# Two middle phases of a four-batch transformer kernel reordered: early maxima, one norm on GpSimd, fillers spread anew

## The reference, cut to what matters

```python
q, k, v = heads(_ln(x) @ Wq + bq), heads(ctx @ Wk + bk), heads(ctx @ Wv + bv)   # 16 heads of 8
x = x + merge(softmax(q @ k.T * 8**-0.5) @ v) @ Wo + bo        # attention 0
h = _ln(x); x = x + relu(h @ Ws1)**2 @ Ws2 + routed(h)         # truncated top-2 weights: routed part is zero save where a weight is 1
x = x + softmax((_ln(x) @ Wq1 + bq1) @ (ctx @ Wk1 + bk1).T) @ (ctx @ Wv1 + bv1)   # attention 1, one head
p = softmax(_ln(x) @ Ws + bs).T                                # 8 experts; each takes its 256 best tokens
x = x + scatter_add(topk(p, 256) * (gelu(xin @ W1 + b1) @ W2 + b2))
```

## Time and profile before

| what | us |
|---|---|
| median of three runs (lowest, highest) | 214.19 (213.75, 217.28) |
| the profiled execution's own time | 214.98 |
| its span | 213.2 |
| busy: TensorE, VectorE, ScalarE, GpSimd | 185.8, 133.1, 90.4, 100.8 |
| mean granted clock of TensorE | 0.983 |

### The profile page before, as it was taken

One profiled execution on the slowest core, in us unless ns is written; L12 is line 12 of the kernel. 1 busy time (PEld: TensorE's weight loads), 2 busy tenths in 40 slices (PEclk: granted clock), 3 DMA queues, 4 the chain that ended last, 5 costly groups with the idle time before them and its releaser, 6 DMA issues.

```text
span 213.2 us, 3647 instructions
## 1 busy us (share of the span) xinstructions
PE 185.8 (87%) x1254; PEld 111.6 (52%) x1254; DVE 133.1 (62%) x457; ACT 90.4 (42%) x219; POOL 100.8 (47%) x111
## 2 busy tenths in 40 slices
PE   6888997997989989899999999799788989987970
PEld 2544542433532556348577675433266867766860
DVE  5787789129791998958778788888742552212110
ACT  2423872242632565134843644356855323333320
POOL 0599638000208002650217748700077887888652
PEclk9999998899999999999999999999999999999996
DMA  6635222101100001049940021110012233323223
GB/s 191 184 82 144 72 51 51 38 8 50 44 0 3 0 0 49 2 143 282 337 134 3 15 88 55 61 40 0 3 44 37 41 48 38 41 39 50 26 29 35
DMA packets 16127, 13.64 MB, mean 64 GB/s; under 512 B 3699, under 2 KB 13079, under 8 KB 16103
## 3 DMA queue, kind: packets, MB, share of 16 engines
q1 hardware_dynamic: 12246, 10.62, 16.4%
q0 software_dynamic: 2944, 2.30, 7.6%
q10 hardware_dynamic: 913, 0.43, 0.8%
HBM read 8.03 MB, written 3.21 MB: 53 GB/s over the span
## 4 chain that ended last, share of the span: by engine, by line
PE 44%; DVE 21%; POOL 12%; issue 9%; DMA 7%; ACT 4%; POOLq 1%; DVEq 0%; ACTq 0%
POOL out L1968 8%; PE psum L1024 8%; DVE mrow L1542 6%; DMA out<-pT,idx 5%; PE psum L921 3%; DVE pT L1689 3%; POOL pT L1960 3%; PE psum L931 3%; PE psum L1042 3%; DVE stats L1424 2%; PE psum L994 2%; PE psum L965 2%; PE psum L947 2%; PE psum L1105 2%; PE psum L1061 2%
## 5 line engine op out<-in xcount | busy, mean ns | idle before, releaser
L1858 POOL TENSOR_SCALAR ve<-mv 128x4 f32<-128x4 f32 (+1 forms) x19 | 4.4, 230 | 72.0 <-DVE mv L1427 71.9
L784 ACT ACTIVATE pT<-psum 103x512 f32<-103x512 f32 (+1 forms) x36 | 21.2, 595 | 31.9 <-PE psum L996 31.8
L1968 POOL DMA_INDIRECT out<-pT,idx x16 | 25.5, 1594 | 8.6 <-issue 4.0
L921 PE MATMUL psum<-c 128*128 128x512 bf16 x108 | 27.6, 379 | 1.0 <-ACT key_map L809 1.0
L1542 DVE TENSOR_REDUCE mrow<-psum 128x8 bf16<-128x616 f32 x32 | 24.6, 789 | 5.0 <-PE psum L965 5.0
L1960 POOL DMA_INDIRECT pT<-gather_rows,idx x16 | 16.9, 1057 | 21.1 <-DVE idx L1747 16.8
L1762 DVE SCALAR_TENSOR_TENSOR pT<-psum,pT 128x128 f32<-128x128 f32 x16 | 5.1, 347 | 26.1 <-PE psum L1380 18.3
L1366 PE MATMUL psum<-xinT,w 128*128 128x256 f32 (+1 forms) x80 | 16.5, 349 | 3.9 <-ACT xinT L866 3.9
L871 ACT ACTIVATE pT<-psum,b 128x256 f32<-128x256 f32 (+1 forms) x40 | 15.0, 431 | 8.2 <-PE psum L1366 7.4
L1380 PE MATMUL psum<-w,pT 128*128 128x128 f32 x128 | 17.7, 284 | 0.6 <-ACT pT L871 0.2
L1569 DVE RECIPROCAL rden<-psum 128x512 f32<-128x512 f32 (+1 forms) x5 | 13.6, 2716 | 6.7 <-PE psum L1024 6.0
(11 more groups left out here) (201 smaller groups left out, 377.4 us busy)
## 6 DMA issues: line engine op xcount, KB each, us to landing
w<-in_L_ffn_W SPq DMA_DIRECT2D x16, 256.0 KB, 6.0
gather_rows<-xrow SPq DMA_DIRECT2D x4, 272.0 KB, 2.1
x<-in_x SPq DMA_DIRECT2D x4, 256.0 KB, 4.1
q_stack<-q_hi SPq DMA_DIRECT2D x32, 32.0 KB, 1.8
out<-res SPq DMA_DIRECT2D x4, 256.0 KB, 2.1
q_stack<-q_lo SPq DMA_DIRECT2D x24, 32.0 KB, 1.8
b_rows<-in_L_ffn_b SPq DMA_DIRECT2D x1, 512.0 KB, 3.9
pT<-gather_rows,idx POOLq DMA_INDIRECT x16
```

Of the source, the lines that this page charges most:

```text
L784: nc.scalar.activation(pT[0:n, b % 2, s, :], ST_ps[s % 2][0:n, :], ACT.Exp).then_inc(exp_done, 1)
L921: pe.matmul(bank[b][:, :], ident16, c16[:, 0:4 * P], start=True, stop=True)
L1968: nc.gpsimd.indirect_dma_start(flat, bass.IndirectOffsetOnAxis(idx[:, h, e:e + 1], 0), y[:, e, h, :], None, bounds_check=last_row, oob_is_ ...
```

## The change

All edits are in the opening and in the phases' order; what is computed stays the same.

- Opening: `prep_q(1)` moves from behind the sixth score piece to behind the eighth and the second turn; fillers 4, 3, 1, 3, 3, 3 before the third to eighth piece; the six at the end go.
- Phase one: two 256-column fillers at slots 10 and 11; VectorE's `ln0_stats(3)` leaves. Six fillers before the last turn that opens phase two.
- Phase two: score pieces 0 and 1 of batch two at slot 0, 2 at slot 1, then 3 to 7 at slots 5, 7, 8, 9, 10, with their maxima in the same slots; three maxima so stand before `normalise`. `ln0_stats(3)` stands behind the first of them. The norm of batch three is GpSimd's (`norm(3)`). `prep_T(3)` and `prep_q(3)` move from slots 1, 2 to 4, 5, `q_low(3)` to slot 6, values to slot 8, `project` and the steps behind it one slot later (`moments2` stays), the once-only products one or two slots later. Fillers: two of 512 columns at slot 3, one at each of 8 to 11.
- Phase three: pieces 0 and 1 at slot 0, 2 at slot 1, 3 to 7 at slots 5, 6, 7, 9, 10; maxima 0 and 1 before `normalise`, the third behind it; values at slot 6; fillers: two of 512 columns at slots 3 and 4, one and two of 256 at slots 9 and 10.

```diff
+HEAD_WARM = {2: 4, 3: 3, 4: 1, 5: 3, 6: 3, 7: 3}
...
+PIECE_SLOTS = {0: {4 + u: (u,) for u in range(PAIRS)},
+               1: {0: (0, 1), 1: (2,), 5: (3,), 7: (4,), 8: (5,), 9: (6,), 10: (7,)},
+               2: {0: (0, 1), 1: (2,), 5: (3,), 6: (4,), 7: (5,), 9: (6,), 10: (7,)}}
+MAXIMA_SLOTS = {0: PIECE_SLOTS[0], 1: PIECE_SLOTS[1], 2: {0: (0, 1), 2: (2,), 5: (3,), 6: (4,), 7: (5,), 9: (6,), 10: (7,)}}
+TURN_SLOTS = {0: {9: (0, 1), 11: (2,)}, 1: {10: (0, 1), 11: (2,)}, 2: {8: (0, 1), 10: (2,)}}
+
+FILL = {0: {}, 1: {3: (2, 7), 8: (1, 4), 9: (1, 4), 10: (1, 4), 11: (1, 4)}, 2: {3: (2, 7), 4: (2, 7)}}
+FILL_HALF = {0: {10: 2, 11: 2}, 1: {}, 2: {9: 1, 10: 2}}
+STEP_SLOTS = {"project": (6, 5, 5), "turn": (7, 6, 6), "hidden": (8, 7, 7), "shared": (10, 9, 9), "moments1": (6, 6, 6), "moments2": (10, 10, 10)}
...
         def prep_slot(b):
-            return 4 if b == 0 else 1
+            return 4
         def values_slot(b):
-            return 2 if b == 0 else 3
+            return (2, 8, 6, 3)[b]
...
-                    warm_head(3)
+                    warm_head(HEAD_WARM[u])
...
-                if u == 5:
-                    prep_q(1)
                 if u % 2 == 1 and u >= 5:
                     maxima_T(0, (u - 5) // 2)
+            prep_q(1)
             maxima_T(0, J - 2)
             pe.wait_ge(ld_neg, 16)
-            warm_head(6)
...
                     if s == 0:
+                        if b == 1:
+                            warm_prep(6)
                         maxima_T(b, J - 1)
...
+                    if b in (1, 2) and s == 0:
+                        scores(b + 1, 0)
...
-                        if b == 1 and s == 4:
-                            pe.wait_ge(once_done, 5)
-                            warm(5, 4)
-                        if s >= 4:
-                            scores(b + 1, s - 4)
...
+                        if s in FILL[b]:
+                            n, to = FILL[b][s]
+                            if to == 4:
+                                pe.wait_ge(once_done, 6)
+                            if to == 7:
+                                pe.wait_ge(mT_done, b + 1)
+                            warm(n, to)
+                        if s in FILL_HALF[b]:
+                            pe.wait_ge(q_lo_done, min(b + 3, B))
+                            pe.wait_ge(v8_done, b + 1)
+                            warm_prep(FILL_HALF[b][s])
+                        for u in PIECE_SLOTS[b].get(s, ()):
+                            if b == 0 or u > 0:
+                                scores(b + 1, u)
+                        for j in TURN_SLOTS[b].get(s, ()):
+                            maxima_T(b + 1, j)
...
-                            if b + 2 < B:
-                                warm(4, 0)
...
-                            if b == 1:
-                                ln0_apply(3)
...
+                        early = b >= 1 and s < 2
+                        if b + 1 < B and early:
+                            for u in MAXIMA_SLOTS[b].get(s, ()):
+                                maxima(b + 1, u)
+                                if (b, u) == (1, 0):
+                                    ln0_stats(3)
+                        t = ph - 1
+                        if t >= 0 and s == 2:
+                            normalise(t, t, 0, J)
+                        if b + 1 < B and not early:
+                            for u in MAXIMA_SLOTS[b].get(s, ()):
+                                maxima(b + 1, u)
+                        if b == 0 and s == prep_slot(b) + 1:
                             q_low(b + 2)
...
-                        if b + 3 < B and s == 8:
-                            ln0_stats(b + 3)
...
+                        if b == 1 and s == step_slot(ph, "moments1"):
+                            q_low(b + 2)
...
+            def norm(b):
+                pool.wait_ge(xnT_ps_done[0], b)
+                pool.wait_ge(rstd_done[0], b + 1)
...
             for ph in range(B):
+                if ph == 1:
+                    ln_rstd(0, 3, 3)
+                    norm(3)
...
-                if ph + 3 < B:
-                    ln_rstd(0, ph + 3, ph + 3)
```

More of the change, by code:

```diff
@@ L62, in halves_done, with step_slot @@
     return n // NG * E * SH + sum(h1 - h0 for _, h0, h1 in GROUPS[:n % NG + 1])
+PIECE_SLOTS = {0: {4 + u: (u,) for u in range(PAIRS)},
[6 more added lines that the diff above has]
+STEP_SLOTS = {"project": (6, 5, 5), "turn": (7, 6, 6), "hidden": (8, 7, 7), "shared": (10, 9, 9), "moments1": (6, 6, 6), "moments2": (10, 10, 10)}
+def step_slot(ph, step):
+    return STEP_SLOTS[step][ph - 1]
 def index_group(e):
@@ L802, in _ @@
                         nc.scalar.copy(b1[:], tail2_ps[:, 0:E * FC]).then_inc(once_done, 1)
-                    if b == 1 and s == 1:
+                    if b == 1 and s == 2:
                         act.wait_ge(once_ps_done, 4)
@@ L815, in _ @@
                     t = ph - 1
-                    if t >= 0 and s == 6:
+                    if t >= 0 and s == step_slot(ph, "turn"):
                         copy_T(1, t, tail1_ps[0])
-                    if t >= 0 and s == 7:
+                    if t >= 0 and s == step_slot(ph, "hidden"):
                         hidden(t, t, 0, J, tail1_ps)
@@ L1203, in _ @@
                         pe.transpose(tail2_ps[:, 0:E * FC], b1_rows[:], ident[0:E * FC, 0:E * FC]).then_inc(once_ps_done, 1)
-                    if b == 1 and s == 0:
+                    if b == 1 and s == 2:
                         pe.wait_ge(once_done, 3)
@@ L1211, in _ @@
                         pe.matmul(tail2_ps[:, P:2 * P], w_q[:, 1, :], centre[:], start=True, stop=True).then_inc(once_ps_done, 1)
-                    if b == 1 and s == 3:
+                    if b == 1 and s == 4:
                         pe.wait_ge(once_done, 4)
@@ L1215, in _ @@
                                   stop=True).then_inc(once_ps_done, 1)
-                    if b == 1 and s == 5:
+                    if b == 1 and s == 6:
                         pe.wait_ge(once_done, 5)
@@ L1219, in _ @@
                                   stop=True).then_inc(once_ps_done, 1)
-                    if t >= 0 and s == 5:
+                    if t >= 0 and s == step_slot(ph, "project"):
                         project(t, 0, J, tail1_ps)
-                    if t >= 0 and s == 6:
+                    if t >= 0 and s == step_slot(ph, "turn"):
                         residual_T(1, t, t, tail1_ps[0])
-                    if t >= 0 and s == 7:
+                    if t >= 0 and s == step_slot(ph, "hidden"):
                         hidden(t, 0, J, tail1_ps)
@@ L1227, in _ @@
                         attend_half(0, s - 5)
-                    if t >= 0 and s == 9:
+                    if t >= 0 and s == step_slot(ph, "shared"):
                         shared(t, 0, J, tail1_ps)
@@ L1604, in _ @@
                                 ln0_apply(2)
-                            if b == 1:
-                                ln0_apply(3)
-                        if b + 1 < B and s >= 4:
-                            maxima(b + 1, s - 4)
-                        if b + 2 < B and s == prep_slot(b) + 1:
+                        early = b >= 1 and s < 2
[11 more added lines that the diff above has]
+                        if b == 0 and s == prep_slot(b) + 1:
                             q_low(b + 2)
@@ L1620, in _ @@
                         t = ph - 1
-                        if t >= 0 and s == 2:
-                            normalise(t, t, 0, J)
-                        if t >= 0 and s == 5:
+                        if t >= 0 and s == step_slot(ph, "project"):
                             add_projection(t, t, 0, J, tail1_ps)
-                        if t >= 0 and s == 6:
+                        if t >= 0 and s == step_slot(ph, "moments1"):
                             stats1(t, t, 0, J)
+                        if b == 1 and s == step_slot(ph, "moments1"):
+                            q_low(b + 2)
                         if ph == B - 1 and s == 8:
                             normalise(B - 1, B - 1, 0, J // 2)
-                        if t >= 0 and s == 9:
+                        if t >= 0 and s == step_slot(ph, "shared"):
                             add_shared(t, t, 0, J, tail1_ps)
-                        if t >= 0 and s == 10:
+                        if t >= 0 and s == step_slot(ph, "moments2"):
                             stats2(t, t, 0, J)
@@ L1901, in _ @@
             ln_rstd(0, 1, 1)
[L1902 to L1906, removed]
+            def norm(b):
+                pool.wait_ge(xnT_ps_done[0], b)
+                pool.wait_ge(rstd_done[0], b + 1)
+                m = moments(0, b)
+                for j in range(J):
+                    ins = nc.gpsimd.tensor_scalar(xn[:, j, :], x[:, b * J + j, :], mv[:, m, j, 0:1], rstd[:, m, j:j + 1],
+                                                  ALU.subtract, ALU.mult)
+                ins.then_inc(xn_done, 1)
+            norm(1)
             pool.wait_ge(q_lo_done, 1)
```

## The result

The changed kernel takes 210.36 us (median of 4, 209.54 to 210.85), the kernel before beside it 215.44 (4 executions). The ratio is 0.986, with a 95% interval of 0.982 to 0.991: faster, by less than two per cent. (The ratio leaves out executions far above the fastest, here the one at 217.28 us, and with them part of those in which the clock fell.) From the medians of what remains, 210.36 against 214.19, one gets 0.982; the interval holds both. I had forecast 209.2 from 214.19, 2.3% less, with a range of 207.9 to 210.8; 0.986 of 214.19 is 211.3, outside it. The first trace of each agrees with the forecast far better than the timed ratio does: spans 208.5 and 213.2, 4.7 us or 2.2% less. What lies between the two is the subject of the experiments.

A forecast was written before the change was run, and what follows sets the result against it. TensorE and VectorE were taken to wait for each other in turn up to the search. Terms 1.0 + 0.3 + 1.7 + 1.7 + 0.3 = 5.0 us off the 214.19 us median gave 209.2, range 207.9 to 210.8.

The forecast's parts named there:

- Step 1: Opening: eight fewer fillers on the path and a later query projection of batch one win 1.0 us (0.8 to 1.15).
- Step 2: End of phase one: VectorE loses the moments, but TensorE's ten added fillers take nearly all back; 0.3 us (0 to 0.5).
- Step 3: Clock fall behind phase one's end goes; 1.7 us won, 0 if the clock falls all the same.
- my slowest sum: All steps at their lower bounds at once: 211.3 us.
- Step 4: Phase two's new order, with an earlier reciprocal and a new wait before the sixth score, wins 1.7 us (0.9 to 2.0).
- The marks: Phase two, from its start: reciprocal at 6.6 us, TensorE at the projection at 13.4; 1.4 us wait before the sixth score.
- The two terms of the sum: Phase two on TensorE: 0.6 us from busy time and 0.85 from idle time, giving 1.45.
- GpSimd's part: Phase two: batch three's norm moved off VectorE to GpSimd, done near 8 us with slack 1.7; wins nothing by itself.
- Step 5: Phase three's new order puts early maxima into VectorE's idle time, with more fillers; wins 0.3 us (-0.5 to 0.8).
- Rival one: Phases two and three: fillers and new waits eat the orders' gain, opening and clock remain; 211.7 us, chance 0.21.
- Rival four: Clock falls elsewhere, as at phase two's slot eight: 212.6 us, or 225 if low to phase three's end; chance 0.08.

The follow-up runs named there:

- e6: Changed kernel with the opening of before put back (query projection of batch one behind the sixth score, old fillers); opening 8.11 us instead of 7.11, ratio 0.991 to before.
- e9: Kernel before, unchanged, traced again; no clock fall in the phases, phase two 28.32 us; no timed ratio.
- e5: Changed kernel with phase two's fifth maximum and query remainder ahead of batch zero's moments on VectorE; phase two 25.08 us instead of 26.50, ratio 0.980 to before.
- e8: Changed kernel with batch three's norm back on VectorE instead of GpSimd; phase two 26.50 us, ratio 0.987 to before.
- e7: Changed kernel with phase three in the order of before, without fillers at slots 3, 4, 9, 10; phase three 26.02 us instead of 25.91, ratio 0.987 to before.
- e4: Changed kernel without its fillers inside phases two and three; phase two 27.89 us, phase three 25.59, ratio 0.987 to before.
- e11: Changed kernel with e5's early fifth maximum and without fillers inside phases two and three; median 208.28 us against 214.18, ratio 0.970 to before.
- e1: Kernel before, unchanged, run again; clock fell at 36 to 40 us, phase two 29.97 us, ratio 1.001.
- e2: Changed kernel, unchanged, timed again; no clock fall in the phases, phase two 26.51 us, ratio 0.990 to before.
- e3: Kernel before with six 256-column fillers ahead of the last turn that opens phase two; phase two 28.31 us, ratio 1.013 to before.
- e10: Kernel before, unchanged, traced again; clock fell at 37 to 41 us, phase two 29.82 us; no timed ratio.

## Why the prediction was right or wrong

- **Step 1, opening: right.** Forecast 1.0, traced 1.0 to 1.1, undone by e6.
- **Step 2, phase one: small and wrong.** Forecast 0.3, traced 0.0 (14.84 and 14.88). The moments' 1.2 us went, and VectorE now waits 0.60 and 0.22 us for TensorE. That the ten fillers took all of it back, the lower end of the step's range, is my reading; no run took them out.
- **Step 3, clock: this failed.** The clock stayed at 1.00 there, with fillers where both waits had been, and against an execution with the fall phase two is shorter by some 1.65 us, as e9 against the first trace shows. That it depends on TensorE's waits was an assumption of mine and is not shown: e9 kept it with 0.26 and 0.95 us of them. And I set the fall down as lost in every execution from a single trace, with "0 if the clock falls all the same" as its only other end; and even that end was left out of the forecast's range: my slowest sum, 211.3, keeps the whole 1.7, and with 0 in its place it is 213.0. By the mean clocks it falls in about 35 of 64 executions of the kernel before, and in three or four of ten of the changed one (0.984 and less; one at 0.987 is not clear). On the mean the term is then about 1.65 times (0.55 less 0.30 to 0.40), an estimate of 0.2 to 0.4 us; against the kernel before at its full clock it is nothing. With 0.3 in place of 1.7 the forecast's own steps give 3.6 us, 210.6; most of what is left to 211.3 is steps 2 and 5.
- **Step 4, phase two: right in size, partly by luck.** Forecast 1.7, traced 28.32 (e9) less 26.50, 1.8. The marks held: reciprocal 6.8 us after the start (forecast 6.6), projection 13.6 (13.4), wait 1.36 (1.4). The two terms of the sum did not: of the 1.8 us TensorE's busy time gave 1.3 (25.8 to 24.5; forecast 0.6) and its idle time 0.5 (2.5 to 2.0; forecast 0.85). That the wait stood on the path is shown by e5. That GpSimd's part wins nothing is shown by e8.
- **Step 5, phase three: nothing instead of 0.3.** The phase is 0.1 shorter and what follows gives it back (e7). Its fillers cost 0.3 of what the order could give (e4, e11).

The sum without the clock was 3.3. The traces at full clock on both sides give 1.1 + 0.0 + 1.8 + 0.1, 3.0 us, by phases. Measured in one piece, from the first query remainder to the first gather, it is 140.4 us in e9 and 137.7 in the changed kernel: 2.7 us or 1.3%, since phase four and what follows it up to the gathers take 63.3 instead of 63.1, where I had forecast equal lengths. The timed executions agree: beside e1 and e2 the kernel before at 0.989 or more has a median of 213.7 (7), the changed kernel at 0.993 or more 211.0 (3), again 2.7. Rival one named the right size (211.7) for the wrong reason: the order's gain came, the clock's did not. Rival four had the clock fall elsewhere, as traced in e4 (52 to 60 us) and e11 (157 to 161), but it looked only at the changed kernel; that the kernel before is not always in the state of its trace was in none of the cases. Its 16 us for 32 at the low clock rest on the 0.50 of the earlier trace rows alone: no run shows such a length, the falls with work of TensorE in them were 3.4 us long (not 3.2), and 6.8 us in e4. The spread of the three executions shown beforehand (213.75 to 217.28 us), and a profiled one with its fall at 214.98, could have told me to ask.

Open: where the changed kernel loses its clock in the executions at 0.984, since no trace caught one; in e11, which differs from it in the two phases only, it was in the experts (157 to 161 us). Open too is why e3's ratio lies 1.3% above 1. In its trace the fall at 86 costs 1.3 us up to the first gather (141.7 against 140.4 in e9), and the rest, from the first gather to the end, took 60.2 us where the first trace of the kernel before had 59.1 and e9 60.1; the six fillers do not reach that stretch.

## What to carry to other kernels

A fall of the clock seen in one trace can be a matter of that execution (here three traces of the kernel before had it and e9 had not): before pricing its removal, look at the granted clock of several executions and multiply by how often it falls. When an order by hand is changed, lay the engines' lines end to end and look for the first instruction that waits behind work it does not need: here the fifth maximum stood behind moments and a remainder, and moving it was worth 1.4 us, as much as half the whole change. Take a wait away before filling it: here the fillers of phases two and three cost 1.1 us (e5 against e11), and with the six of e3 the clock was 1.00 from 34 to 39 us and fell at 86.

## What the runs showed of the hardware that was not expected

- The same program, with the same waits of 0.26 and 0.95 us, had a clock of 1.00 behind them in e9 and fell to 0.50 in the first trace, e1 and e10.
- By the clock column, a fall was about 3.4 us at 0.50 of the full clock (first trace, e1, e10, e3, e11) and cost 1.5 to 1.65 at the start of phase two; in e4 it was about 6.8 us at 0.50, between 52 and 60.
- VectorE's norm of 128 by 512 elements took longer the more GpSimd worked during it: 1.11 us with GpSimd idle (7.33 us in the changed kernel), 1.51 with 0.70 us of its work, 2.46 with 1.61 (20.38 us in the changed kernel), 2.87 with 2.02, 3.95 with 3.36 (e8). Reciprocals of 128 by 512 elements that read a bank stayed at 3.34 to 3.36: 3.36 in the changed kernel with GpSimd busy throughout (40.52) and with it idle (64.95), 3.34 with it idle in e8 (42.49).
- The start of the opening's maxima moved between executions: VectorE's first remainder started between 11.2 us (e4) and 14.8 (e10). Part of it is the length of TensorE's work: the four unread products of 512 columns near 5 us took 1.03 us in e4 and 1.91 in e10, the projection's two 1.10 and 1.59, though the clock column says 1.00 in both. The stretch from the first gather to the end took 58.5 us (e6, e8) to 61.7 us (the longest, e11's, with the fall at 157 in it). Neither is part of the change, and each spread is larger than any step of the sum.
